# An adapter kernel on one core: its opening laid out anew, with three loading queues, two batches side by side and the sort on one partition

## The reference

```python
h = jnp.einsum('bsh,bhk->bsk', hidden_states, W_down[role]) + b_down[role][:, None, :]
h = jax.nn.gelu(h, approximate=False)
u = jnp.einsum('bsk,bkh->bsh', h, W_up[role]) + b_up[role][:, None, :]
y = hidden_states + u
mean = jnp.mean(y, axis=-1, keepdims=True)
var = jnp.mean(jnp.square(y - mean), axis=-1, keepdims=True)
yn = (y - mean) * jax.lax.rsqrt(var + LN_EPS)
return yn * gamma[role][:, None, :] + beta[role][:, None, :]
```

## Time and profile before

| quantity | value |
|---|---|
| median of three runs | 1440.74 us |
| the profiled execution, its own time | 1440.42 us |
| its span on the core | 1438.4 us |
| TensorE busy | 1403.1 us (98%) |
| VectorE, ScalarE, GpSimd busy | 1202.3, 775.5, 155.0 us |
| DMA | 286.94 MB, mean 199 GB/s |

### The profile page before, as it was taken

How to read it: one execution, slowest core, us unless ns; L and a number is a source line. 1 busy time by engine, 2 the same in 40 slices (tenths; PEclk the granted TensorE clock), 3 DMA queues, 4 the chain that set the end, 5 groups by cost and what they waited for, 6 DMA issues and landing times.

```text
span 1438.4 us, 32063 instructions
## 1 busy us (share of the span) xinstructions
PE 1403.1 (98%) x6154; PEld 1157.6 (80%) x6155; DVE 1202.3 (84%) x1445; ACT 775.5 (54%) x2051; POOL 155.0 (11%) x212
## 2 busy tenths in 40 slices
PE   4899999999999999999999999999999999999997
PEld 3688888888888888888888878888888888888886
DVE  4689888888888888888888889888888888888888
ACT  3355555555555555555555555555555555555555
POOL 0667000000000000000000277400000000000000
PEclk9999999999999999999999999999999999999999
DMA  8887666666656666656665788766566566556653
GB/s 223 236 245 225 193 193 199 191 187 200 196 181 196 202 183 195 199 185 187 207 190 182 237 250 232 208 200 201 182 196 202 182 196 198 184 190 204 189 189 141
DMA packets 210886, 286.94 MB, mean 199 GB/s; under 512 B 25456, under 2 KB 156656, under 8 KB 210864
## 3 DMA queue, kind: packets, MB, share of 16 engines
q1 hardware_dynamic: 205232, 272.79, 61.8%
q0 software_dynamic: 5632, 13.90, 3.8%
HBM read 185.93 MB, written 100.66 MB: 199 GB/s over the span
## 4 chain that ended last, share of the span: by engine, by line
PE 92%; DMA 2%; DVE 2%; DVEq 1%; issue 1%; SPq 1%; ACT 1%
PE p_up L693 15%; PE p_down L693 15%; PE p_up L695 15%; PE p_down L695 15%; PE p_up L694 15%; PE p_down L694 15%; DMA h_dram<-h 1%; DVEq L208 1%; DMA h_quad<-h_dram 0%; DVE row L565 0%; DMA row<-in_L_cond_W_up 0%; DVE xT_raw L513 0%; DMA role_col<-in_itok_B 0%; SPq L235 0%; DVE hT_lo L538 0%
## 5 line engine op out<-in xcount | busy, mean ns | idle before, releaser
L693 PE MATMUL p_down<-wd_hi,xT_hi 128*128 x1024 | 401.6, 392 | 17.4 <-DVE xT_lo L518 17.4
L694 PE MATMUL p_down<-wd_lo,xT_hi 128*128 x1024 | 400.6, 391 | 0.0
L695 PE MATMUL p_down<-wd_hi,xT_lo 128*128 x1024 | 400.4, 391 | 0.0
L693 PE MATMUL p_up<-wu_hi,hT_hi 128*128 x1008 | 392.5, 389 | 1.2 <-DVE hT_lo L538 1.2
L695 PE MATMUL p_up<-wu_hi,hT_lo 128*128 x1008 | 392.2, 389 | 0.0
L694 PE MATMUL p_up<-wu_lo,hT_hi 128*128 x1008 | 392.2, 389 | 0.0
L408 ACT ACTIVATE hT_hi<-p_hT 128x512 fp32r<-128x512 f32 x126 | 75.6, 600 | 407.1 <-DVE p_hT L532 407.1
L565 DVE SCALAR_TENSOR_TENSOR row<-p_up,row 128x1024 f32<-128x1024 f32 x126 | 154.3, 1224 | 153.2 <-PE p_up L695 144.5
L693 PEld LDWEIGHTS p_down<-wd_hi,xT_hi 128*128 128x128 f32 x1024 | 193.5, 189 | 59.9 <-issue 19.9
L423 ACT ACTIVATE xT_hi<-xT_raw 128x1024 fp32r<-128x1024 f32 x127 | 134.8, 1062 | 181.6 <-PE p_down L695 141.6
L695 PEld LDWEIGHTS p_down<-wd_hi,xT_lo 128*128 128x128 f32 x1024 | 193.8, 189 | 40.8
(11 more groups left out here) (90 smaller groups left out, 894.2 us busy)
## 6 DMA issues: line engine op xcount, KB each, us to landing
x_quad<-in_x SPq DMA_DIRECT2D x512, 128.0 KB, 3.4
row<-in_x SPq DMA_DIRECT2D x126, 512.0 KB, 3.9
out<-row SPq DMA_DIRECT2D x126, 512.0 KB, 2.8
h_dram<-h SPq DMA_DIRECT2D x128, 256.0 KB, 3.8
h_quad<-h_dram SPq DMA_DIRECT2D x512, 64.0 KB, 2.0
w_raw<-in_L_cond_W_down POOLq DMA_DIRECT2D x64, 64.0 KB, 4.3
w_raw<-in_L_cond_W_up POOLq DMA_DIRECT2D x64, 64.0 KB, 2.7
row<-in_L_cond_W_down SPq DMA_DIRECT2D x16, 128.0 KB, 3.7
```

What stands on the lines that cost most here:

```text
L693: pe.matmul(dst, a_hi, w_hi, start=first, stop=False)
L694: pe.matmul(dst, a_hi, w_lo, start=False, stop=False)
L695: return pe.matmul(dst, a_lo, w_hi, start=False, stop=last)
```

## The change

1. The roles are loaded once, as one row on one partition. VectorE makes the key on that row, counts roles 2 and 1, and takes the eight largest keys with one MAX; from them come the numbers of the first batches (`first_numbers`), without the table. TensorE spreads the key over all partitions and into a column, and one more matmul gives the sorted numbers.
2. The other rows of the table (offsets, due counts) are worked out by GpSimd on partition 0 from the counts, in 27 instructions, most of which wait for the one before. `rows_ready` tells when they are done. The sort can also put role 1 or a small role elsewhere; for this input (no role 0, many of 1 and 2) its order and its loading plan are those of before.
3. Three queues load. ScalarE issues pieces 0 and 1 as its first instructions, SyncE the roles, x of batches 0 and 1, then pieces 2 and 3, then x of 2; GpSimd the bias and pieces 4 to 7, of which each waits until the piece two before has landed, then b_up, gamma and beta, each of which waits for the one before it.
4. Batches 0, 1 and 2 are transposed, rounded and subtracted by halves of four blocks. TensorE multiplies first half of 0, first half of 1, second half of 0, second half of 1, then the two halves of 2, then up 0, whose order of loops is turned (by block outside, halves of columns inside, a wait for piece 4 + c at each block). Batch 1 goes into p_up[1].
5. The order on all engines up to batch 3 is written out by hand; the loops begin after it.

```diff
+            sp.dma_start(role_row, role.rearrange("(o b) -> o b", o=1)).then_inc(roles_loaded, 16)
...
+            sp.wait_ge(first_known, 1)
+            for b in range(2):
+                load_quads(sp.value_load(first_numbers[0:1, b:b + 1], min_val=0, max_val=B - 1), b)
+            load_first(sp, FD - 2)
+            load_first(sp, FD - 1)
+            sp.wait_ge(numbers_ready, 1)
+            sp.wait_ge(rows_ready, 1)
+            load_x(2)
...
+            store_h(0)
+            load_x(3)
+            load_h(0)
+            store_h(1)
+            load_h(1)
+            load_x(4)
+            store_h(2)
+            sp.wait_ge(first_raw[FD + FU - 1], 16 * NQ)
+            load_row(0, 0, 0)
+            load_row(1, 0, 1)
...
+            def step(*group):
+                for ins in group:
+                    ins.then_inc(rows_step, 1)
+                done[0] += len(group)
+                pool.wait_ge(rows_step, done[0])
...
+            step(pool.tensor_scalar(past_gate, index_row[0:1, :], one(P_GATE), None, ALU.is_ge),
+                 pool.tensor_scalar(past_mid, index_row[0:1, :], one(P_END), None, ALU.is_ge))
+            step(pool.tensor_tensor(slot, past_gate, past_mid, ALU.subtract),
...
+            pool.wait_ge(first_raw[FD - 2], raw_once)
+            load_bias(R - 1, 0)
+            for n in range(FD, FD + FU):
+                pool.wait_ge(first_raw[n - 2], raw_once)
+                pool.wait_ge(first_split, n - RING + 1)
+                load_first(pool, n)
+            pool.wait_ge(first_raw[FD + FU - 2], raw_once)
+            load_params(R - 1, 0, 16)
...
+            round_half(1, 1)
+            gelu(0)
+            round_half(2, 0)
+            round_half(2, 1)
+            round_first(4)
+            round_first(5)
+            gelu(1)
+            round_h(0)
+            round_first(6)
+            round_x(3)
+            gelu(2)
+            round_first(7)
...
+            chain(dve.max(first_keys[:, :], key))
+            chain(dve.tensor_copy(first_ints[:, :], first_keys[:, :]))
+            dve.tensor_scalar(first_numbers[:, :], first_ints[:, :], P - 1, P - 1, ALU.bitwise_and,
+                              ALU.bitwise_xor).then_inc(first_known, 1)
...
+            subtract_half(1, 1)
+            dve.wait_ge(rows_ready, 1)
+            params_at = [look_up(dve, PARAMS_AT, b, 0, PARAMS) for b in range(4)]
+            when_loaded = [look_up(dve, WHEN_LOADED, b, 16, 16 * R) for b in range(4)]
+            dve.wait_ge(bias_loaded, when_loaded[0])
+            bias_h(0, params_at[0], p_down[:, :])
+            transpose_half(2, 0)
+            transpose_half(2, 1)
+            subtract_half(2, 0)
+            subtract_half(2, 1)
+            split_first(4)
+            split_first(5)
+            dve.wait_ge(bias_loaded, when_loaded[1])
+            bias_h(1, params_at[1], p_up[1][:, 0:K])
+            transpose_h(0)
+            subtract_h(0)
+            split_first(6)
+            transpose_x(*seq(0, 3, 0))
+            split_x(3)
+            dve.wait_ge(bias_loaded, when_loaded[2])
+            bias_h(2, params_at[2], p_down[:, :])
+            split_first(7)
...
+            pe.wait_ge(rows_ready, 1)
...
+            weights_at = [look_up(pe, WEIGHTS_AT, b, 0, HC * K) for b in range(3)]
+            when_split = [look_up(pe, WHEN_SPLIT, b, 1, (R - 1) * (DN + UN) + 1) for b in range(3)]
...
+            half_product(0, 0, p_down[:, :], weights_at[0]).then_inc(half_down, 1)
...
+            half_product(1, 0, other, weights_at[1]).then_inc(half_down, 1)
+            pe.wait_ge(x_lo_ready, 1)
+            half_product(0, 1, p_down[:, :], weights_at[0]).then_inc(down_done, 1)
+            pe.wait_ge(x_lo_ready, 2)
+            half_product(1, 1, other, weights_at[1]).then_inc(down_done, 1)
...
+            pe.wait_ge(h_lo_ready, 1)
+            for c in range(KC):
+                pe.wait_ge(first_split, FD + c + 1)
+                for n in range(NH):
```

494 lines of the change are left out of this document (313 added, 181 removed).

## The result

The change makes the kernel slower: 1445.78 us, median of 8 runs (1442.80 to 1448.04), against 1440.57 of the kernel before in the same series (8 runs, 1439.27 to 1443.51). Ratio 1.0032, 95% interval 1.0019 to 1.0045. The forecast was 1435.2 with a range up to 1440.5.

A forecast was written before the change was run, and what follows sets the result against it. TensorE, busy 98% of 1438.4 us, was the bound, leaving only the opening to win. Down 3 starting at 49.9 instead of 55.36 gains 5.5: span 1432.9, execution 1434.9, median 1435.2 us, range 1431 to 1440.5.

The forecast's parts named there:

- X: Start of down 3 on TensorE, after the same 96 matmuls in both kernels; forecast 49.9 us instead of 55.36.
- look-ups of TensorE: Six table look-ups ahead of TensorE's first product, 0.6 us each and the first 0.9: 4.0 us, start at 17.3.
- The first x: Opening loads: role row in at 3.1 us, x 0 issued at 7.6 and transposed at 12.1 instead of 13.72.
- The table, a new wait on the path: GpSimd's 27 instructions ahead of TensorE's first product: 8.5 us from 4.8, done at 13.3 (bounds 10.6 to 15.5).
- the table is the bound: Rival on GpSimd's chain: at 0.52 us an instruction the gain is gone, from 0.63 slower by over 0.2%; chance 0.08.
- The table is held up by VectorE: Rival: GpSimd waits out two VectorE subtractions, making the table 1.9 us later and the time 1437.1; chance 0.14.
- VectorE's look-ups ahead of the first bias add: Eight look-ups in VectorE's sequencer, about 21.3 to 26.5 us, claimed hidden before batch 0's bias add.
- The trip of h 0: Batch 0's h stored at 29.7, landed 3.8 us later at 33.5, loaded and transposed another 3.8 later at 37.3.
- the rest costs nothing: Pieces 0 and 1 on ScalarE's queue, later parameter rows and role 1's weights were claimed to add no time.
- The stop in up 0, and what is late behind h 0: TensorE stands about 3 us inside up 0, before its last six matmuls, waiting for the split of piece 7.
- T + 12.6: Down 3's start counted from T, the transpose of batch 0's h, forecast at 37.3 us instead of 42.42.
- Nothing new behind X: TensorE after down 3 starts: the remaining 1383.04 us were claimed to be left alone, with no new waits.

The follow-up runs named there:

- e2: The change with one wait in place of the eight behind GpSimd's last nine table instructions; 1445.89 us, ratio 1.0037 to the kernel before.
- e11: e10 with TensorE waiting for only 20 of the 27 table instructions and VectorE for 22; 1441.60 us, ratio 1.0003 to the kernel before.
- e10: e9 plus e1's edit, which equals e6 with the table and its look-ups put back; 1444.22 us, ratio 1.0025 to the kernel before.
- e6: e5 with weight pieces 4 to 7 issued on SyncE's queue instead of GpSimd's; 1434.95 us, ratio 0.9964 to the kernel before.
- e3: The change with constants for the first batches, no table wait or look-ups until the loops; leaves out a case; 1440.11 us, ratio 0.9998.
- e1: The change with VectorE's steps 4 to 7 reusing registers read once instead of new look-ups; 1446.73 us, ratio 1.0042 to the kernel before.
- e4: The change with piece 7 rounded and split before x 3 and the bias and Gelu of batch 2; 1446.59 us, ratio 1.0047.
- e8: The change with e1's and e6's edits and e7's order, table and early look-ups kept; 1442.33 us, ratio 1.0012 to the kernel before.
- e9: The change with pieces 4 to 7 on SyncE's queue alone, table kept; 1444.62 us, ratio 1.0031 to the kernel before.
- e12: e11 with TensorE's and VectorE's look-ups for batches after 0 moved to later, ahead of their use; 1437.81 us, ratio 0.9977.
- e13: e12 with b_up, gamma and beta of the first batches fetched only once h 0 is transposed; 1433.99 us, ratio 0.9956.
- e14: e12 with the load of x 3 issued behind the load of h 0; 1437.27 us, ratio 0.9974 to the kernel before.
- e15: e12 with the edits of both e13 and e14; 1434.88 us, ratio 0.9958 to the kernel before.
- e7: e6 with pieces 6 and 7 rounded and split ahead of h 0; 1439.26 us, ratio 0.9991 to the kernel before.
- e16: e13 with e7's order, pieces 6 and 7 split ahead of h 0; 1435.46 us, ratio 0.9965 to the kernel before.
- e5: e3 and e1 together: no table wait at the start, VectorE's extra look-ups gone; 1438.80 us, ratio 0.9984 to the kernel before.

## Why the prediction was wrong

The forecast was on the wrong side. Its account was right in form: a start X, and a long rest that the change leaves nearly alone. Span and X were forecast as 1432.9 and 49.9 and came as 1442.2 and 56.76. (The median missed by 10.6, since the profiled execution was 1.6 below it; the forecast had taken 0.3 for this.) The 9.3 us divide so:

| step of the prediction | forecast | came | adds to the error |
|---|---|---|---|
| table ready | 13.3 | 16.82 | 3.5 |
| look-ups of TensorE | 4.0 | 4.4 | 0.4 |
| first product to store of h 0 | 12.4 | 12.9 | 0.5 |
| store to load | 3.8 | 3.9 | 0.1 |
| load to transpose | 3.8 | 5.6 | 1.8 |
| transpose to down 3 | 12.6 | 13.2 | 0.6 |
| behind X | 0 | 2.4 | 2.4 |

- **The first x: right, and better.** The role row had landed at 2.13 (forecast 3.1), x 0 was transposed at 10.39 (12.1). Nothing came of it, since TensorE waited for the table.
- **"The table, a new wait on the path": this step failed.** The mechanism was named rightly, the size was not. It was worked out as 17 dependent starts at 0.36 us and 9 free ones at 0.08, and 0.15 more for each of the eleven rows. Measured, the eleven one-number instructions ahead of the rows start 0.34 apart on average (3.35 to 7.11) whether or not they depend on each other, and the eleven rows of 128 columns take 0.69 each on average (7.11 to 14.70) where 0.51 (dependent) and 0.23 (free) were taken. The rows cost 3.1 us more than forecast, the numbers 1.9. The chain took 13.5 us instead of 8.5; it began 1.5 sooner than forecast, so 3.5 remained. e2 shows that taking the waits away saves next to nothing, e11 that shortening what TensorE waits for pays, e10 against e6 that table and look-ups together cost 9 us where the pieces come over SyncE's queue (5.7 in e3, where they come over GpSimd's). This step is the largest, but with it alone the forecast would have been 1438.7, still below the kernel before: the other side of 1440.57 is reached only with the trip and the loss behind X. The rival **"the table is the bound"** said that at 0.52 us an instruction the gain is gone. It came to 0.50, in a chain that began 1.5 sooner, and it had been given 0.08. The small instruction in the earlier trace rows gave one duration and one delay, and no pace at which such instructions follow each other.
- **"The table is held up by VectorE": in part.** L390 took 1.71 us, beside VectorE's subtraction of piece 0 at 7.10, while L391 of the same form took 0.61: 1.1 us. The forecast for this case had 1.9 in two places. That is also what the Trainium skill says in "SBUF — State Buffer", section "Who interferes with whom": a VectorE instruction with two SBUF inputs and a GpSimd instruction that reads SBUF block one another. These two rows agree, 1.71 against 0.61. In e6 the table's last five numbers took 3.18 us instead of 2.12: VectorE's split of piece 2 started at 16.57, while they ran, and in the change at 17.18, behind their end. So the table's length also depends on when x and the pieces land, and in the kernels that keep the table's instructions and the six look-ups as they are (e1, e4, e8, e9, e10) the first product came between 21.69 and 22.92.
- **VectorE's look-ups ahead of the first bias add: "hidden" was wrong.** They were put at 21.3 to 26.5 and ran from 26.9 to about 32, since the subtraction ahead of them waits for TensorE's first half product. From the end of down 0 to the store it took 2.5 us (31.5 to 34.07) where 1.5 were forecast. TensorE was 0.6 quicker than forecast through down 0, so that the table above shows only 0.5.
- **The trip of h 0: store right, load not.** 3.8 was taken from the steady part "since traffic is then like that of the steady part". It was not: x 3 was issued at 35.18, between store and load, and was not counted, and the parameter rows, issued at 31.84 and 37.92, were said to "come one at a time" and costed at nothing. Against the transfers of e12 (10.3 us) those without the parameter rows beside them were 2.8 us shorter (e13) and those without x 3 ahead of them 3.5 (e14). How the 1.8 of the change divide between them was not tried. In the median the parameter rows cost 3.0 us (e12 to e13) or 2.4 (e14 to e15), x 3 nothing that shows. The forecast of "the rest costs nothing" looked only at when the rows were needed, not at what they met on the way. The Trainium skill, "Trainium Kernel Development and Optimization", section "Key Constraints", says that DMAs of the several queues are served by one set of engines; the share of 0.97 against 0.62 in the same stretch of e12 and e13, with the parameter rows on GpSimd's queue and h 0 on SyncE's, agrees.
- **The stop in up 0, and what is late behind h 0: right.** About 3 us ahead of the last six matmuls were forecast, 2.50 came, put down to the split of piece 7. T + 12.6 was forecast for down 3, and in the thirteen kernels that keep the order of piece 7 it starts 13.0 to 13.8 us behind the transpose of h 0. A new order alone wins little: in e4 and e7 what is moved past makes down 4 wait for 3.5 and 5.6 us, in e16, where that wait is short, the median is no lower, and only in e8 against e10 is it lower, by 1.9 us.
- **"Nothing new behind X": wrong by 2.4 in the profiled execution.** In the kernels that keep the order of piece 7 it runs from -0.8 (e1) to +4.0 (e12); in e4 and e7 it is 8.0 and 8.4, since the stop stands behind X there. VectorE's additional look-ups in steps 4 to 7, three a step, were not counted at all, although the changed code has them; they make gaps of 0.4 us ahead of the ups. Their price in the median is below what e1, e5 and e10 resolve. In e12, whose profiled execution was the slowest of its eleven, some 1.6 us of the offset arise between 800 and 1000 us, when the last role's weights come: 869 matmuls there against 876 before, 7 at 0.23. What decides this from run to run is open.

Was the table all of it? No. e3 takes 8.2 us from the first product and gives 5.7 in the median; e11 has the first product nearly where the forecast had it (18.42 against 17.3) and is still at 1441.6. Only with the parameter rows out of the way (e13) or the pieces sooner (e6) do the times reach what was forecast, 1434.0 and 1434.95 against 1435.2, and in both the first product starts sooner than was forecast, at 15.79 and 12.89.

## What to carry to other kernels

A chain of tiny instructions is priced by its number, at the pace of the engine that runs it (here 0.3 to 0.7 us each), and not by one duration or by its waits; before such a chain goes ahead of the first product, let each reader wait for the part that it reads, and let it read only what it needs next (e11 and e12: 6.4 us for a few lines). A transfer that nobody waits for still has a price when it meets one that somebody waits for: move it behind, as in e13. A quicker transfer is worth nothing once the engine that takes it has work of its own until then, as in e15. An early start is worth what the next wait leaves of it, here from 0.3 (e8 to e7) over 0.7 (e3) and 0.8 (e10 to e12) to 0.9 (e10 to e6) of each microsecond, so ask at once what is late next.

## What the runs showed of the hardware

- On GpSimd an instruction on one number occupied 0.34 to 0.42 us of the chain and one on 128 columns of one partition 0.43 to 0.65, waited for or not (2.60 with four waits, 2.58 without). Beside VectorE's subtractions it was more: 1.71 once, and 3.18 instead of 2.12 for five numbers.
- A value read from SBUF into a register cost TensorE's sequencer 0.7 us, of which 0.3 was the load, and six in a row did not overlap. VectorE's eight took 5.15 us.
- A queue of its own doesn't make a trip short: the same 256 KB stored and loaded over SyncE's queue took from 6.5 (e15) to 14.1 us (e5) from the issue of the store to the landing of the load's last quarter, depending on what else was fetched.
- TensorE fell to the lower of its two levels, 1.2 GHz, behind some stops and not behind others of the same length: in e12 it restarted at 32.13 behind 3.38 idle at a granted clock of 0.58 over 30 to 35 us, in e13 at 32.84 behind the same 3.38 at 1.00. The runs of one kernel here span 3 to 7 us, which the mean granted clock of the run does not explain: the slowest run of the change, 1448.04 us, has 0.997 and its fastest, 1442.80, 0.995. What does is open.
